# Routing logits with the gate as stationary operand, and combine weights turned in 32x32 blocks by VectorE

## The chip, the cores and the metric

The kernel runs on one core of one Trainium2 chip. The metric is the device time of one execution in microseconds (us); the value of a kernel is the median of its runs. A profile is one further execution, of which the hardware profiler keeps a trace with every instruction. The engines are called by the profile's names: PE is TensorE's matrix multiplications and PEld its weight loads, DVE is VectorE, ACT is ScalarE, POOL is GpSimd, and SP is SyncE, whose queue (SPq) issues most of the DMAs.

## The reference, cut to what matters

Eight sequences (B = 8) of 512 tokens (S) and 256 features (D) go through an attention layer and then through a mixture of 16 experts (E) with a hidden width of 128. Eight experts are kept for each token, and one shared expert is always added. What the change touches is the routing, here without the rest:

```
x = x + xattn(ctx_2048, layernorm(x), ...)
xf = layernorm(x)
logits = l2norm(xf) @ l2norm(gate_w).T        # 4096 tokens x 16 experts
scores = sigmoid(logits)
topk_scores, topk_idx = top_k(scores, 8)
combine = scores of the top 8 / their sum, 0 for the other experts
routed = sum over e of combine[:, e] * ((silu(xf @ w_gate[e]) * (xf @ w_up[e])) @ w_down[e])
out = x + routed + silu(xf @ sw_gate) * (xf @ sw_up) @ sw_down
```

## The kernel before

Every engine walks one list of steps, ORDER, and does its own part of each step; semaphores tie the engines together. The list is written out by hand: attention() gives each step a time by which the list is sorted, and order() appends the second half.

The first half is the attention: 16 groups of four heads (two groups for each sequence). A group's scores are computed twice on PE (L732 for the maxima, which DVE reduces at L1201, and L748 for the exponentials, which ACT takes at L868 into e_buf). POOL adds up the exponentials at L1407. The routing of sequence 0 and the first six expert units lie among the last groups.

The second half is the experts: units n = 0, 1, ... run over TODO, that is over 8 sequences b and 17 experts e (e = 16 is the shared one). A unit has a step gate_up (12 matmuls of 128x512 on PE, L840 through the helper at L653, into PSUM banks ps0 to ps3) and a step down (6 matmuls into pst). The step down of unit n stands behind gate_up of unit n + 2 (LAG = 2). In between, ACT computes silu into sg, DVE multiplies (L1304, and L1315 with the combine weight from CB), ACT rounds the product to hh (L868), and DVE takes the remainder hl (L1317). The operands are float32 kept as two float32r parts, a high one and a low one, so each product takes three matmuls.

The routing of sequence b + 1 is spread over the units of sequence b. After gate_up of e = 9 and 10 PE turns the normalized x (turn_x2), and X2h and X2l hold it with features on partitions. After gate_up of e = 12 PE computes the logits (L809 to L812), with 128 tokens of x as the stationary operand and the 16 or 32 gate columns moving. The 16 small DVE steps "gating" (N_GATE) follow: six of them after gate_up of e = 12, six after e = 13, the rest after e = 14. They put the two parts of the logits together (L1258, L1262), scale them (L1267), wait for ACT's tanh (L1270), find the eight largest (L1273, L1276), and leave the combine weights in LG, 128 tokens on partitions by 4 x 16. After gate_up of e = 15, the step turn_c turns LG on PE (four transposes), copies it with ACT to CT [16, 512], and SP stores CT to the scratch tensor in HBM with one DMA. From there, load_c brings one expert's row of 512 weights to all 128 partitions of a buffer of CB, of which there are NC = 4. The first four loads for a sequence stand right behind turn_c. A load of unit m waits until the DVE has used buffer m - 4.

For sequence 0 the same steps lie among the attention's groups 14 and 15, one at a time between other steps.

PSUM banks go round in rings: RING3 (three banks, first half) and RING2 (banks 4 and 5, second half) hold the steps that need a bank of their own; turn_c was one of them.

## Time and profile before

| | |
|---|---|
| device time, median of 3 runs | 1065.49 us (1064.21 to 1065.64) |
| span of the profiled execution, first to last instruction | 1056.2 us |
| PE busy | 1012.5 us, 96% of the span |
| DVE busy | 647.5 us, 61% |
| ACT busy | 465.9 us, 44% |
| POOL busy | 389.0 us, 37% |
| mean granted TensorE clock | 0.992 |

The profiled execution has no device time of its own on record, so its span is set beside the median of the runs: 9.3 us of the device time lie outside the span. A busy share is an average over both halves of the kernel. What the change is worth must be read in each half: where PE never waits, its own instructions set the time, and where it waits, the engine that it waits for does.

### The profile page before, as it was taken

How to read it: one execution, taken by the hardware profiler on the slowest of the kernel's cores; microseconds unless marked ns; L12 is line 12 of the kernel's file. 1: busy time of each engine (PE TensorE's matmuls, PEld its weight loads, DVE VectorE, ACT ScalarE, POOL GpSimd, SP SyncE). 2: the span in 40 equal slices, each digit the busy share in tenths (PEclk: the TensorE clock that was granted, in tenths of full speed). 3: DMA queues.
4: the chain of work that ended last, by engine and by line, in shares of the span. 5: the costliest groups of instructions: out<-in, count | busy, mean ns of one | idle time of the engine just before them, and what ended most of it. 6: DMA issues, size and time to landing. Idle time of an engine off the chain costs nothing.

```text
span 1056.2 us, 14941 instructions
## 1 busy us (share of the span) xinstructions
PE 1012.5 (96%) x5198; PEld 773.3 (73%) x5198; DVE 647.5 (61%) x1469; ACT 465.9 (44%) x865; POOL 389.0 (37%) x355
## 2 busy tenths in 40 slices
PE   4789999999999998899999999999999999999998
PEld 3656767676767665567888888888888888888886
DVE  5877777877777557355565555555555555555544
ACT  3346565656665646545323323333333333332322
POOL 3379797879797967345210010010010100100000
PEclk9899999999999999999999999999999999999999
DMA  7343433434333223324222121121220230221220
GB/s 239 104 131 78 131 81 111 108 84 131 73 110 75 65 65 105 92 86 131 75 80 61 52 80 50 61 81 40 72 80 31 71 90 20 91 80 31 93 68 20
DMA packets 65674, 87.87 MB, mean 83 GB/s; under 512 B 10720, under 2 KB 31088, under 8 KB 65600
## 3 DMA queue, kind: packets, MB, share of 16 engines
q1 hardware_dynamic: 63680, 84.83, 28.0%
q10 hardware_dynamic: 1920, 2.10, 0.6%
q8 instruction: 41, 0.67, 0.3%
q14 instruction: 33, 0.27, 0.1%
HBM read 56.97 MB, written 4.46 MB: 58 GB/s over the span
## 4 chain that ended last, share of the span: by engine, by line
PE 91%; DVE 4%; ACT 2%; SPq 1%; issue 1%; DMA 1%; POOL 0%; DVEq 0%; ACTq 0%
PE ps L653 50%; PE pst L653 18%; PE ps L732 6%; PE ps L759 5%; PE pst L748 5%; PE ps L659 4%; PE ps L772 1%; DVE mx L1201 1%; ACT e_buf L868 1%; SPq L606 1%; PE ps L811 1%; SPq L541 1%; ACT ctx_h L868 0%; DVE wsrc_l L1148 0%; PE ps L812 0%
## 5 line engine op out<-in xcount | busy, mean ns | idle before, releaser
L653 PE MATMUL ps<-x_h,weights 128*128 128x512 f32 x1088 | 365.6, 397 | 1.4 <-DVE x L1194 0.8
L653 PEld LDWEIGHTS ps<-x_h,weights 128*128 128x128 f32 x1088 | 204.5, 188 | 51.8 <-issue 1.0
L1201 DVE TENSOR_REDUCE mx<-ps 128x1 f32<-128x512 f32 x256 | 173.3, 685 | 81.8 <-PE ps L732 80.9
L868 ACT ACTIVATE hh<-qb 128x512 fp32r<-128x512 f32 x136 | 86.0, 632 | 296.4 <-DVE qb L1315 273.7
L653 PE MATMUL ps<-x_l,weights 128*128 128x512 f32 x544 | 214.6, 395 | 0.0
L653 PE MATMUL pst<-hh,weights 128*128 128x512 f32 x544 | 194.6, 399 | 0.0
L1304 DVE TENSOR_TENSOR qb<-ps,sg 128x512 f32<-128x512 f32 x136 | 94.1, 692 | 160.2 <-PE ps L653 153.8
L868 ACT ACTIVATE e_buf<-pst 128x512 f32<-128x512 f32 x256 | 147.4, 596 | 92.8 <-PE pst L748 81.8
L1317 DVE TENSOR_TENSOR hl<-qb,hh 128x512 fp32r<-128x512 f32 x136 | 94.3, 693 | 95.0 <-ACT hh L868 95.0
L1407 POOL TENSOR_TENSOR e_sums<-e_sums,e_buf 128x1024 f32<-128x1024 f32 x60 | 143.5, 2391 | 7.2 <-ACT e_buf L868 1.2
L1359 POOL TENSOR_SCALAR ve<-mv 128x4 f32<-128x4 f32 x8 | 1.8, 226 | 347.1 <-DVE mv L1242 347.1
L653 PEld LDWEIGHTS ps<-x_l,weights 128*128 128x128 f32 x544 | 102.1, 188 | 24.6
L748 PE MATMUL pst<-q_stack,k_stack 98*128 98x512 f32 x256 | 108.4, 425 | 12.1 <-ACT e_buf L868 12.0
L868 ACT ACTIVATE sg<-ps 128x512 f32<-128x512 f32 x136 | 81.1, 596 | 86.6 <-PE ps L653 86.6
L653 PEld LDWEIGHTS pst<-hh,weights 128*128 128x128 f32 x544 | 102.2, 188 | 23.3 <-DVE hl L1317 0.8
L732 PE MATMUL ps<-k_stack,q_stack 97*128 97x512 f32 x256 | 109.7, 430 | 6.7 <-DVE mx L1201 6.2
L653 PE MATMUL pst<-hl,weights 128*128 128x512 f32 x272 | 107.3, 394 | 0.0
L1315 DVE TENSOR_TENSOR qb<-qb,cb 128x512 f32<-128x512 f32 x124 | 87.4, 705 | 4.2
L1407 POOL TENSOR_TENSOR e_sums<-e_buf 128x1024 f32<-128x1024 f32 x30 | 71.8, 2394 | 48.8 <-PE ps L772 48.3
L732 PEld LDWEIGHTS ps<-k_stack,q_stack 97*128 97x128 f32 x256 | 49.2, 193 | 46.0 <-issue 29.1
L748 PEld LDWEIGHTS pst<-q_stack,k_stack 98*128 98x128 f32 x256 | 49.4, 194 | 27.1 <-ACT e_buf L868 16.6
L759 PE MATMUL ps<-e_buf,v_buf 128*32 128x512 f32 x512 | 62.1, 603 | 0.0
(159 smaller groups left out, 1391.5 us busy)
## 6 DMA issues: line engine op xcount, KB each, us to landing
cb<-combine_scratch SPq DMA_DIRECT2D x128, 256.0 KB, 3.2
q_stack<-q_h SPq DMA_DIRECT2D x128, 64.0 KB, 2.0
k_stack<-k_h SPq DMA_DIRECT2D x124, 64.0 KB, 2.0
ctx_raw<-in_ctxT SPq DMA_DIRECT2D x7, 1024.0 KB, 5.2
q_stack<-q_l SPq DMA_DIRECT2D x64, 64.0 KB, 2.0
out_x<-ob SPq DMA_DIRECT2D x16, 256.0 KB, 2.2
k_stack<-k_l SPq DMA_DIRECT2D x62, 64.0 KB, 2.0
x<-in_x SPq DMA_DIRECT2D x7, 512.0 KB, 6.5
```

The costliest lines, as they stand in the source:

```text
L541: e.dma_start(f32(KS[g % 2][at:at + 32, h, :]), f32(src[32 * h:32 * h + 32, :])).then_inc(sem(f"stack{g % 2}{h}"), 16)
L653: ins = engine.matmul(dst, lhsT, rhs, start=start and n == 0, stop=stop and n == len(terms) - 1)
L659: ins = engine.transpose(dst, src, ID[0:k, 0:k])
L732: engine.matmul(ps, QS[z][0:97, h, 128 * q:128 * q + 128], KS[z][0:97, h, :], start=True, stop=True).then_inc(sem("s_max"), 1)
L748: engine.matmul(YP[:, m % 2, :], KS[z][0:98, h, 128 * k:128 * k + 128], QS[z][0:98, h, :], start=True, stop=True).then_inc(sem("s_t"), 1)
L759: ins = engine.matmul(OP[32 * i:32 * i + 32, :], VB[:, b % 2, k, hh + i, :], EB[:, SLOTS[8 * g + 4 * (i // 2) + k], i % 2, :], start=k == ...
L868: return engine.activation(dst, src, func, **kw)
L1201: engine.tensor_reduce(MX[:, g % 2, h // 2, h % 2, q:q + 1], bank(step), AX.X, ALU.max).then_inc(sem("max"), 1)
L1304: engine.tensor_tensor(QB[:, w, :], GP[n][1], SG[:, w, :], ALU.mult).then_inc(sem("hq"), 1)
L1315: engine.tensor_tensor(QB[:, w, :], QB[:, w, :], CB[:, m % NC, :], ALU.mult).then_inc(sem("hc"), 1)
L1317: engine.tensor_tensor(HLB[:, n % NH, :], QB[:, w, :], f32(HHB[:, n % NH, :]), ALU.subtract).then_inc(sem("h_lo"), 1)
L1407: engine.tensor_tensor(ES[:, a, :, :], first, EB[:, SLOTS[n + 1 + i], :, :], ALU.add).then_inc(sem("e_add"), 1)
```

## The change

The logits are now computed with the gate as the stationary operand: GT holds four copies side by side of the 32 columns (16 high parts, 16 low parts), 128 columns in all, and the 512 tokens of a sequence move. That is four matmuls of 128x512 instead of sixteen of 128x32 or 128x16. The result has the gate's columns on partitions, four times over, and the tokens along the free axis. Four DVE transposes in 32x32 blocks, one for each group of 32 partitions, each read a quarter of the tokens and put them on partitions in LT; one DVE addition joins the high and the low part. That makes 19 gating steps instead of 16, and since the steps are handed out six at a time after e = 12, 13 and 14, one is left for e = 15.

The step turn_c loses its PE transposes and its ACT copy. One DVE transpose in 32x32 blocks turns LG into CT [128, 2, 32] instead, and because the blocks leave the experts of different token blocks on different partitions, SP stores CT with eight DMAs in place of one, in runs of 32 numbers (128 bytes). The loads from the scratch tensor are as before, but wait for all eight stores. The gate's rows, as loaded, now lie in a free part of shift_rows.

```diff
@@ sizes, rings, tiles
-N_LN1, N_LN2, N_GROWS, N_GATE = N_SMALL1 + 4, N_SMALL2 + 4, 3 + rsqrt_steps(1) + 3, 16
+N_LN1, N_LN2, N_GROWS, N_GATE = N_SMALL1 + 4, N_SMALL2 + 4, 3 + rsqrt_steps(1) + 3, 19
-         if s[0] in ("q", "y", "shift", "turn_x", "turn_s", "turn_r", "turn_x2", "turn_c", "bo")
+         if s[0] in ("q", "y", "shift", "turn_x", "turn_s", "turn_r", "turn_x2", "bo")
-         if s[0] in ("turn_x2", "turn_c", "store") or (s[0] == "gating" and s[2] == 0)]
+         if s[0] in ("turn_x2", "store") or (s[0] == "gating" and s[2] == 0)]
-        GT = sb("gate_t", [128, 2, 2, E], F32R)
+        GT = sb("gate_t", [128, 2, 4, 2, E], F32R)
-        CT = s2("ct", [E, S])
+        LT, CT = s2("lt", [128, 4, 2 * E]), s2("ct", [128, 2, 32])
@@ SyncE
                     sp.wait_ge(sem("ct"), b + 1)
-                    engine.dma_start(cscr[b], CT[:, :]).then_inc(sem("st_ct"), 16)
+                    for r in range(4):
+                        for c in range(2):
+                            at = 32 * r + E * c
+                            engine.dma_start(cscr[b].rearrange("e (a c r t) -> e a c r t", a=2, c=2, r=4)[:, :, c, r, :],
+                                             CT[at:at + E, :, :]).then_inc(sem("st_ct"), 16)
@@ TensorE
-                    lp = own_bank(step)[:, 0:8 * E].rearrange("p (q e) -> p q e", q=4)
-                    for q in range(4):
-                        tok = slice(128 * q, 128 * q + 128)
-                        both = GT[:, :, :, :].rearrange("p k a e -> p k (a e)")
-                        engine.matmul(lp[:, q, :], X2h[:, b % 2, 0, tok], both[:, 0, :], start=True, stop=False)
-                        for k in range(2):
-                            engine.matmul(lp[:, q, 0:E], X2l[:, b % 2, k, tok], GT[:, k, 0, :], start=False, stop=False)
-                        ins = engine.matmul(lp[:, q, :], X2h[:, b % 2, 1, tok], both[:, 1, :], start=False, stop=True)
+                    lp = own_bank(step)
+                    for k in range(2):
+                        four = GT[:, k].rearrange("p f a e -> p (f a e)")
+                        engine.matmul(lp, four, X2h[:, b % 2, k, :], start=k == 0, stop=False)
+                        ins = engine.matmul(lp, four, X2l[:, b % 2, k, :], start=False, stop=k == 1)
                     ins.then_inc(sem("logit"), 1)
-                elif kind == "turn_c":
-                    b = step[1]
-                    pe.wait_ge(sem("gating"), N_GATE * (b + 1))
-                    ps = own_bank(step)
-                    turns([(ps[0:E, 128 * q:128 * q + 128], LG[:, q, :]) for q in range(4)], sem("c_t"))
@@ ScalarE
-                elif kind == "turn_c":
-                    b = step[1]
-                    act.wait_ge(sem("c_t"), b + 1)
-                    if b > 0:
-                        act.wait_ge(sem("st_ct"), 16 * b)
-                    copy(CT[:, :], bank(step)[0:E, :]).then_inc(sem("ct"), 1)
@@ VectorE
-                    if i == 0:
-                        lp = bank(step)[:, 0:8 * E].rearrange("p (q a e) -> p q a e", q=4, a=2)
-                        dve.wait_ge(sem("logit"), b + 1)
-                        if b > 0:
-                            dve.wait_ge(sem("c_t"), b)
-                        engine.tensor_copy(LG[:, :, :], lp[:, :, 1, :]).then_inc(done, 1)
-                    elif i == 1:
-                        lp = bank(("gating", b, 0))[:, 0:8 * E].rearrange("p (q a e) -> p q a e", q=4, a=2)
-                        dve.wait_ge(done, base + 1)
-                        engine.tensor_tensor(LG[:, :, :], lp[:, :, 0, :], LG[:, :, :], ALU.add).then_inc(done, 1)
+                    if i < 4:
+                        r = slice(32 * i, 32 * i + 32)
+                        lp = bank(("gating", b, 0)).rearrange("p (q r t) -> p q r t", q=4, r=4)
+                        if i == 0:
+                            dve.wait_ge(sem("logit"), b + 1)
+                        engine.transpose(LT[r, :, :], lp[r, :, i, :]).then_inc(done, 1)
+                    elif i == 4:
+                        dve.wait_ge(done, base + 4)
+                        engine.tensor_tensor(LG[:, :, :], LT[:, :, 0:E], LT[:, :, E:2 * E], ALU.add).then_inc(done, 1)
...
+                elif kind == "turn_c":
+                    b = step[1]
+                    dve.wait_ge(sem("gating"), N_GATE * (b + 1))
+                    if b > 0:
+                        dve.wait_ge(sem("st_ct"), 128 * b)
+                    engine.transpose(CT[:, :, :], LG[:, :, :].rearrange("p (a c) e -> p a (c e)", a=2)).then_inc(sem("ct"), 1)
```

Three places show what moves in the lists of the engines. The first is DVE in the second half, at the routing of sequence 1, before the change, from the unit e = 14 to the unit e = 15 (qb, hh and hl are the unit's products, cb the combine weight, lg the logits and later the weights):

```order
L1317 TENSOR_TENSOR hl<-qb,hh 128x512 [waits h_hi]
L1278 TENSOR_REDUCE ts_57<-t_56 128x4
L1281 RECIPROCAL ts_57<-ts_57 128x4 [waits gating]
L1283 TENSOR_TENSOR sc<-sc,rep 128x64
L1286 TENSOR_TENSOR lg<-sc,ts_57 128x64 [waits gating]
L1304 TENSOR_TENSOR qb<-ps,sg 128x512 [waits h_lo,silu,gu]
L1315 TENSOR_TENSOR qb<-qb,cb 128x512 [waits ld_cb3,hq]
L1317 TENSOR_TENSOR hl<-qb,hh 128x512 [waits h_hi]
```

The same place of DVE in the changed kernel:

```order
L1272 TENSOR_TENSOR sc<-sc,rep 128x64
L1299 TENSOR_TENSOR qb<-ps,sg 128x512 [waits h_lo,silu,gu]
L1310 TENSOR_TENSOR qb<-qb,cb 128x512 [waits ld_cb3,hq]
L1312 TENSOR_TENSOR hl<-qb,hh 128x512 [waits h_hi]
L1275 TENSOR_TENSOR lg<-sc,ts_57 128x64 [waits gating]
L1282 STREAM_TRANSPOSE ct<-lg 128x64 [waits st_ct,gating]
L1299 TENSOR_TENSOR qb<-ps,sg 128x512 [waits h_lo,silu,gu]
```

The last gating step has moved behind the unit e = 15, and the turn stands behind it.

The second place is SP's queue behind that step, before the change:

```order
L628 DMA combine_scratch<-ct 16x512 [waits ct]
L635 DMA cb<-combine_scratch 128x512 [waits hc,st_ct]
```

And in the changed kernel, at the routing of sequence 0, the same two steps (the next four rows of the queue, word for word):

```order
L629 DMA combine_scratch<-ct 32x1x32 [waits ct]
L629 DMA combine_scratch<-ct 32x1x32 x7
L637 DMA cb<-combine_scratch 128x512 [waits st_ct]
L637 DMA cb<-combine_scratch 128x512 x3
L551 DMA w_raw<-in_wg 128x2x128 [waits w_lo]
```

Seven more stores stand in front of the first load.

The third place is DVE at the routing of sequence 0, in the attention's last but one group, before the change (mx is a maximum of scores, ru the reciprocals of the sums, rn the scale of the logits):

```order
L1258 COPY lg<-ps 128x64 [waits logit]
L1262 TENSOR_TENSOR lg<-ps,lg 128x64 [waits gating]
L1201 TENSOR_REDUCE mx<-ps 128x1 [waits s_max]
L1267 TENSOR_TENSOR lg<-lg,rn 128x64 [waits ln2,gating]
L1207 RECIPROCAL ru<-ps 128x16 [waits spread,s_turned]
L1270 TENSOR_SCALAR sc<-sc 128x64 [waits tanh]
```

The same place in the changed kernel:

```order
L1248 STREAM_TRANSPOSE lt<-ps 32x128 [waits logit]
L1248 STREAM_TRANSPOSE lt<-ps 32x128
L1190 TENSOR_REDUCE mx<-ps 128x1 [waits s_max]
L1248 STREAM_TRANSPOSE lt<-ps 32x128
L1196 RECIPROCAL ru<-ps 128x16 [waits spread,s_turned]
L1248 STREAM_TRANSPOSE lt<-ps 32x128
L1251 TENSOR_TENSOR lg<-lt 128x64 [waits gating]
L1190 TENSOR_REDUCE mx<-ps 128x1 [waits s_max]
L1256 TENSOR_TENSOR lg<-lg,rn 128x64 [waits ln2,gating]
L1259 TENSOR_SCALAR sc<-sc 128x64 [waits tanh]
```

The addition that joins the two parts read one operand from PSUM and now reads both from SBUF (lt), and a reduction stands between it and the scaling.

## Rows read from the trace of the kernel before

**Rows 1.** Windows: stretch, length, then busy us of PE, PEld, DVE, ACT, POOL; PEclk.

```profile
478.00:1050.00 572.00, 572.00 (x2589) 463.92 (x2588) 315.50 (x617) 192.13 (x336) 47.96 (x134) 1.00 0.21 66
```

**Rows 2.** Timeline, routing of sequence 0: start, us, engine, line, instruction, idle before.

```profile
410.55 2.35 POOL L1407 TENSOR_TENSOR e_sums<-e_sums,e_buf 128x1024 f32<-128x1024 f32 x1
...
411.18 1.80 DVE L1267 TENSOR_TENSOR lg<-lg,rn 128x64 f32<-128x64 f32 x1
412.86 1.27 POOL L1431 TENSOR_TENSOR weights<-w_raw,weights 128x512 fp32r<-128x512 f32 x1
...
413.01 0.26 ACT L868 ACTIVATE sc<-lg 128x64 f32<-128x64 f32 x1 [2.43 <-DVE lg L1267]
...
413.90 0.59 PE L748 MATMUL pst<-q_stack,k_stack 98*128 98x512 f32 x1 [2.46 <-ACT e_buf L868]
...
419.69 0.81 DVE L1286 TENSOR_TENSOR lg<-sc,ts 128x64 f32<-128x64 f32 x1
```

**Rows 3.** Timeline of PE, logits of sequence 7.

```profile
955.08 0.39 PE L653 MATMUL ps<-x_h,weights 128*128 128x512 f32 x1
...
957.01 0.48 PE L653 MATMUL pst<-hh,weights 128*128 128x512 f32 x1
957.33 0.39 PE L653 MATMUL pst<-hl,weights 128*128 128x512 f32 x1
```

**Rows 4.** Timeline of PE, turning the combine weights of sequence 7.

```profile
969.44 0.39 PE L653 MATMUL ps<-x_h,weights 128*128 128x512 f32 x1
969.67 0.60 PE L659 MATMUL ps<-ident_sb,lg 128*16 128x128 f32 x4
...
970.34 0.40 PE L653 MATMUL pst<-hl,weights 128*128 128x512 f32 x1
```

**Rows 5.** Groups by line and form, DVE: busy us, mean ns, idle before.

```profile
L1304 DVE TENSOR_TENSOR qb<-ps,sg 128x512 f32<-128x512 f32 x136 | 94.1, 692 | 160.2 <-PE ps L653 153.8 <-ACT sg L868 5.8
...
L1262 DVE TENSOR_TENSOR lg<-ps,lg 128x64 f32<-128x64 f32 x8 | 1.8, 224 | 0.3
...
L1258 DVE COPY lg<-ps 128x64 f32<-128x64 f32 x8 | 1.8, 219 | 1.0 <-PE ps L812 1.0
```

**Rows 6.** Timeline of DVE, first units of sequence 7.

```profile
979.42 0.69 DVE L1315 TENSOR_TENSOR qb<-qb,cb 128x512 f32<-128x512 f32 x1
980.82 0.69 DVE L1317 TENSOR_TENSOR hl<-qb,hh 128x512 fp32r<-128x512 f32 x1 [0.70 <-ACT hh L868]
...
987.09 0.69 DVE L1304 TENSOR_TENSOR qb<-ps,sg 128x512 f32<-128x512 f32 x1 [0.78 <-PE ps L653]
```

**Rows 7.** Timeline of all engines, the end of the routing of sequence 7.

```profile
969.87 0.69 DVE L1304 TENSOR_TENSOR qb<-ps,sg 128x512 f32<-128x512 f32 x1 [0.69 <-PE ps L653]
...
971.86 0.57 ACT L868 ACTIVATE ct<-ps 16x512 f32<-16x512 f32 x1
```

**Rows 8.** Timeline of SP's queue, the loads that follow.

```profile
974.03 14.82 SPq L635 DMA_DIRECT2D cb<-combine_scratch  x7
```

**Rows 9.** DMA issues: KB each, median us from issue to landing.

```profile
cb<-combine_scratch SPq DMA_DIRECT2D x128, 256.0 KB, 3.2
...
out_x<-ob SPq DMA_DIRECT2D x16, 256.0 KB, 2.2
...
combine_scratch<-ct SPq DMA_DIRECT2D x8, 32.0 KB, 1.6
```

**Rows 10.** Line 641, the output's stores: issue ns min/median/max, first and last start.

```profile
L641 SPq DMA_DIRECT2D out_x<-ob x16: 388/389/389, 543.2 to 1053.6; - x16
```

**Rows 11.** Line 628, the store of CT, the same columns.

```profile
L628 SPq DMA_DIRECT2D combine_scratch<-ct x8: 317/318/341, 422.5 to 972.5; - x8
```

**Rows 12.** Line 606, copies into the stacks, the same columns.

```profile
L606 SPq DMA_DIRECT2D q_stack<-q_h x128: 507/590/1601, 22.5 to 403.6; - x128
```

**Rows 13.** Timeline of all engines, the first combine weights of sequence 0.

```profile
425.48 1.77 SPq L635 DMA_DIRECT2D cb<-combine_scratch  x4
...
432.89 0.69 DVE L1309 SCALAR_TENSOR_TENSOR qb<-qb,cb 128x512 f32<-128x512 f32 x1
```

More of the change, by code:

```diff
@@ L477, in bank_free @@
             if kind == "gating":
-                return sem("gating"), N_GATE * s[1] + 2
-            if kind == "turn_c":
-                return sem("ct"), COUNT[s]
+                return sem("gating"), N_GATE * s[1] + 4
             return sem("o_add"), COUNT[s]
@@ L988, in scalar_program @@
                     gb = bank(step)[:, 0:2 * E].rearrange("p (k e) -> p k e", k=2)
-                    copy(GT[:, :, 0, :], gb).then_inc(sem("gate_hi"), 1)
+                    four = gb.rearrange("p k (f e) -> p k f e", f=1).to_broadcast([128, 2, 4, E])
+                    copy(GT[:, :, :, 0, :], four).then_inc(sem("gate_hi"), 1)
                 elif kind == "second_starts":
@@ L1232, in vector_program @@
                         dve.wait_ge(sem("gate_hi"), 1)
-                        engine.tensor_tensor(GT[:, :, 1, :], gb, f32(GT[:, :, 0, :]), ALU.subtract).then_inc(sem("gate_lo"), 1)
+                        four = gb.rearrange("p k (f e) -> p k f e", f=1).to_broadcast([128, 2, 4, E])
+                        engine.tensor_tensor(GT[:, :, :, 1, :], four, f32(GT[:, :, :, 0, :]), ALU.subtract).then_inc(sem("gate_lo"), 1)
                 elif kind == "ln2" and (step[2] < 8 or 10 <= step[2] < 12):
@@ L1270, in vector_program @@
                         engine.tensor_scalar(SC[:, :, :], SC[:, :, :], 0.5, 0.5, ALU.mult, ALU.add).then_inc(done, 1)
-                    elif i < 8:
-                        dve.wait_ge(done, base + 4)
-                        engine.max(T8[:, i - 4, :], SC[:, i - 4, :]).then_inc(done, 1)
-                    elif i < 12:
-                        dve.wait_ge(done, base + 8)
-                        engine.match_replace(REP[:, i - 8, :], T8[:, i - 8, :], SC[:, i - 8, :], 0.0).then_inc(done, 1)
-                    elif i == 12:
+                    elif i < 11:
+                        dve.wait_ge(done, base + 7)
+                        engine.max(T8[:, i - 7, :], SC[:, i - 7, :]).then_inc(done, 1)
+                    elif i < 15:
+                        dve.wait_ge(done, base + 11)
+                        engine.match_replace(REP[:, i - 11, :], T8[:, i - 11, :], SC[:, i - 11, :], 0.0).then_inc(done, 1)
+                    elif i == 15:
@@ L1278, in vector_program @@
                         engine.tensor_reduce(TS8[:, :, :], T8[:, :, :], AX.X, ALU.add).then_inc(done, 1)
-                    elif i == 13:
-                        dve.wait_ge(done, base + 13)
+                    elif i == 16:
+                        dve.wait_ge(done, base + 16)
                         engine.reciprocal(TS8[:, :, :], TS8[:, :, :]).then_inc(done, 1)
-                    elif i == 14:
+                    elif i == 17:
                         engine.tensor_tensor(SC[:, :, :], SC[:, :, :], REP[:, :, :], ALU.subtract).then_inc(done, 1)
-                    elif i == 15:
-                        dve.wait_ge(done, base + 15)
+                    elif i == 18:
+                        dve.wait_ge(done, base + 18)
```

16 lines of the change are left out of this document (8 added, 8 removed).

## The prediction

> **What bounds the kernel now.** I read the windows of the trace first, because the busy shares of the page are means over two different halves. In the experts' half PE is busy for 572.00 of 572.00 us, at a granted clock of 1.00 (the 2.4 GHz level); DVE is busy for 55% and ACT for 34% of it [rows 1]. So in this half time is worth what PE's own instructions cost, and work on another engine is free as long as PE does not come to wait for it. Then I read the timeline around the change's places. The reader is to look at distances between starts, not at durations: matmuls overlap, and a packed 128x512 matmul starts 0.23 us after the one before it, although its row says 0.39. At sequence 0 the kernel is another: there, in the attention, PE waited 2.46 us at 413.90 us, and the wait leads through ACT's tanh (which waited 2.43 us, and behind which the exponentials stand in ACT's order) to DVE's scaling of the logits, which took 1.80 us [rows 2].
>
> **The logits on PE, experts' half.** Between the last full matmul of the unit e = 12 (start 955.08) and the second one behind the logits (957.33) lie 2.25 us [rows 3]. Two packed steps take 0.47 of that, so the sixteen small matmuls cost 1.78 us, 0.11 each: none is paid by its 16 or 32 columns. They become four matmuls of 128x512, the same shape and types as the experts' (x parts moving, 128 stationary columns), and 4 x 0.233 = 0.93 us. Gain: 0.85 us.
>
> **The turn on PE.** From 969.44 to 970.34 us are 0.90 us for four transposes and two packed steps [rows 4]: 0.43 us, all of which goes. Together 1.28 us for each sequence. Seven of the eight sequences (1 to 7) are routed in the half where PE never waits: 7 x 1.28 = 9.0 us.
>
> **DVE, experts' half.** The trace shows no DVE transpose. Below, its price is bounded by the copy from PSUM of half the elements, 219 ns for 128x64. From that and the 692 ns of 128x512 [rows 5] comes a slope of 1.06 ns per element of a partition, so 128 elements a partition would take 0.29 us; above I take the whole 692 ns. A cost by elements is the natural reading of these rows, and I use 0.29: four make 1.15 us, against the copy and the addition that go (0.44 us). The new addition and the turn of LG are 128x64 (0.22 us each). Net 1.15 us more for a sequence. After e = 12 the chain of six steps is then 1.15 + 2 x 0.22 and some gaps, about 1.7 us. A unit lasts 4.2 us: L1315 of e = 0 starts at 979.42 and L1304 of e = 2 at 987.09 [rows 6], and with the 0.69 us of the L1304 ahead of L1315 [rows 5] two units make 8.4 us. DVE, waiting for ACT in the middle, is tied up from 978.70 (that L1304) to 981.51 (the end of hl), 2.8 us of it. So 1.4 us are left per unit, 0.93 more where the logits run, and the tanh for ACT falls about when silu of the next unit is due. What overruns is a few tenths and is late only for hq and hl, which PE needs late: down of a unit starts behind gate_up of the unit after next, at about 986.9 us for the product whose hl ends at 981.51 [rows 6]. That cover is 5.4 us. With 0.69 us for a transpose the overrun is 1.6 us more, still under it. ACT loses its copy of 0.57 us [rows 7]. I cost all of this at nothing.
>
> **The store and the loads, experts' half.** This is the longest new chain. Before, CT was ready at 972.43, 2.56 us after the start of the product of e = 15 at 969.87 [rows 7], and the first loads were issued at 974.03 [rows 8]. Landing 3.2 us later [rows 9] makes 977.2, and the first use is at 979.42 [rows 6]: 2.2 us to spare, 1.8 once PE's turn is gone. Now the last gating step and the turn stand behind hl of e = 15 (2.8 us, then 2 x 0.22 and gaps): CT is ready at about 3.4, that is 0.85 us later. Eight issues take seven more of them: by the output's stores, also SBUF to HBM with three dimensions, 0.39 us [rows 10] and 0.03 between them (my choice, as the rows show none back to back), 2.9 us; the ends are the old store's own 0.32 us [rows 11] and the 0.59 us of the copies into the stacks [rows 12]. Landing: 2.2 instead of 1.6 us [rows 9], ends 1.6 and the double of 2.2. The weights come 0.85 + 2.9 + 0.6 = 4.35 us later and DVE waits 2.6 us for them, at L1315's place of e = 0. Ends: 0.85 + 2.45 = 3.3 us later (a wait of 1.5) and 0.85 + 4.3 + 2.8 = 7.9 (a wait of 6.1). Behind the waiting product stand hl, the next unit's product, and on ACT hh and the next silu; PE waits for hl only after 5.4 us. So the expected wait of 2.6 us is paid off over two units by the 1.4 us that each has left, and costs nothing; the high end costs 0.7 us a sequence, 5 us in all.
>
> The Trainium skill speaks against exactly this part: its page "DMA: Bandwidth & Descriptors" (section Specifications) says that transfers under 512 B are done as read-modify-write, and the new runs have 128 B. It gives no duration for such a store, so it would add an unknown time to the landing, and the sum stays as it is unless that passes the cover; no row here shows such a store.
>
> **Sequence 0.** Here DVE is on the path. The scaling (128x64, both operands in SBUF) ran from 411.18 to 412.98, eight times its usual 0.22 us, and ended when POOL's addition of 410.55 + 2.35 = 412.90 did [rows 2]. The addition before it, which reads PSUM, took its usual 224 ns (its group's mean [rows 5]) although POOL ran as well. After the change both the addition and the scaling read only SBUF. The addition would then end with POOL's instruction at 412.9, the reduction behind it takes 0.69, and the scaling meets POOL's next instruction, which ends at 412.86 + 1.27 = 414.13 [rows 2]: the logits are ready at about 414.3 instead of 412.98, and PE's wait ends 1.3 us later. The 0.85 us that the logits save lies ahead of this wait and only lengthens it; the 0.43 us of the turn is behind it and counts. Net +0.9 us. Ends: -1.3, if the additions fall between POOL's instructions and PE's whole saving counts, and +4, if one more of the DVE steps that follow meets a POOL addition of 2.35 us and another of 1.27. The weights for unit 0 need no more time than there is: from the end of lg at 420.50 [rows 2], a reduction and the turn make about 421.4, the stores and their landing 2.9 + 0.4 + 2.2, so 426.9 instead of the loads' issue at 425.48, landing 430.1 to 430.5; the use is at 432.89 [rows 13].
>
> The Trainium skill's page "SBUF — State Buffer" (section SBUF: two separate sides) has the rule: VectorE with two SBUF inputs and GpSimd share one port pair, and the loser is blocked for the whole instruction. The row of 1.80 us agrees. [...]
>
> **Sum.** -9.0 + 0.9 = -8.1 us. The profiled span is 1056.2 us, and 9.3 us lie around it up to the median of the runs, 1065.5; the change does not touch these. 1065.5 - 8.1 = **1057.4 us**, a ratio of 0.992.
>
> **The rivals.**
> 1. *The weights come late.* The chain of eight stores passes the cover, and PE waits in every sequence. For it: seven issues in one queue, short runs. Against it: the dearest of the three issues shown has a median of 0.59 us, and the two stores to HBM land after 1.6 and 2.2 us [rows 9, 12]. The cover ends when the weights come 1.8 + 5.4 = 7.2 us later than now; each us beyond that costs 7 us, so the gain of 8.1 is gone at 8.4 us later. With 9.5 us: 7 x 2.3 = 16 us, 1057.4 + 16 = 1073.5. This is the rival on the other side. 6%.
> 2. *Sequence 0 pays more.* The lock between DVE and POOL hits several steps, PE waits 3 to 6 us more there: 1060 to 1063.5 us. The chain at 411 to 414 us speaks for it, and the next POOL instructions leave few gaps. 14%.
> 3. *Sequence 0 pays nothing*: PE's saving counts eight times and the steps fall into gaps. 1065.5 - 10.3 = 1055.2 us. 15%.
> 4. *The transpose is slow*, at or above 0.69 us: absorbed in the experts' half, but sequence 0 gets 4 x 0.4 = 1.6 us more on its path: 1059 us. 10%.
> 5. *The change doesn't save on PE*: matmuls that read the fourfold gate do not run at 0.23 us. Nothing in the profile says so, since the experts' matmuls have the same shape. With twice the price (0.47 us each) the logits cost what they did, and 3 us remain from the turn: 1063.4 us. 4%.
>
> **How the numbers follow.** The forecast's own case, with sequence 0 between 0 and +2 us, has 51% and lies at 1056.3 to 1058.8. Rivals 2, 3 and 4 border on it. Leaving out rivals 1 and 5 and the far tail of 2 leaves out under 2 in 10: 1054.6 to 1062.0. A measurement of this kernel tells about 0.2% (2.1 us) from no change. Faster by more than that takes all cases but rival 1, half of 5 and the last of 2: 0.90. Within it 0.04, slower 0.06.
>
> **What the profile of the changed kernel would show.** Right: PE packed in the experts' half, four 128x512 matmuls 0.23 us apart in each routing and no matmul for the turn; the half shorter by 9.0 us. DVE transposes of 0.29 us. At e = 0 of each sequence DVE waits about 2.6 us for the DMA of cb, and PE does not wait for hl. At sequence 0 a scaling or an addition of over 1 us beside a POOL instruction. It would be wrong if PE's waits list hl or qb in the experts' half, if issues of the new stores take over 0.7 us, or if the wait at sequence 0 grows past 4 us.

## The result, and the profile after

The changed kernel takes 1091.34 us (median; 1089.9 to 1094.46) against 1064.85 us (1063.19 to 1065.64) for the kernel before on the same chip: a ratio of 1.0263, 95% interval 1.0237 to 1.0289. The prediction said 1057.4 us and faster; the kernel is 26.5 us slower. What happened is rival 1 in kind, the weights come late and PE waits in every sequence, but from a smaller lateness than rival 1 asked for: it let PE wait only when DVE waits longer than 5.4 us for the weights, and DVE waited 4.0 us on average (5.6 at sequence 1).

I read the waits of the experts' half first, since the forecast stood on PE not waiting there. In the kernel before, PE was busy for all of [rows 1]. After:

```profile
DVE qb L1310 <- DMA cb<-combine_scratch: 27.9, 7, 5.6
...
PE pst L655 <- DVE yt L1320: 22.5, 7, 5.1
```

(Waits: engine, line, what it waited for, us in total, times, longest.) DVE waits seven times for the combine weights, 4.0 us each (predicted: 2.6), and PE waits seven times, 3.2 us each, for something that the prediction never named: yt, the copy of the *finished* sequence's output out of PSUM. (The load of PE's weights for the same step, on PEld, is put down to hl, 25.4 us in 7. At sequence 7 that hl is the one of unit 1, which ended at 1022.09 and which down of e = 0 doesn't need; the hl that it needs had ended at 1019.38.) (Lines have moved: L655, L1299, L1310, L1312 and L1320 are the L653, L1304, L1315, L1317 and L1325 of before; L629 stores CT, L637 loads the weights.)

The timeline shows how the two waits hang together. These are the last unit of routing for sequence 7 and the first units of sequence 7, of the changed kernel:

```profile
1004.50 0.69 DVE L1299 TENSOR_TENSOR qb<-ps,sg 128x512 f32<-128x512 f32 x1 [0.53 <-PE ps L655]
...
1007.48 0.25 DVE L1282 STREAM_TRANSPOSE ct<-lg 128x64 f32<-128x64 f32 x1
1007.76 4.99 SPq L629 DMA_DIRECT2D combine_scratch<-ct  x8
...
1012.89 0.69 DVE L1299 TENSOR_TENSOR qb<-ps,sg 128x512 f32<-128x512 f32 x1 [2.11 <-PE ps L655]
1013.94 10.43 SPq L637 DMA_DIRECT2D cb<-combine_scratch  x7
1017.30 0.69 DVE L1310 TENSOR_TENSOR qb<-qb,cb 128x512 f32<-128x512 f32 x1 [3.72 <-DMA cb<-combine_scratch]
...
1018.69 0.69 DVE L1312 TENSOR_TENSOR hl<-qb,hh 128x512 fp32r<-128x512 f32 x1 [0.70 <-ACT hh L862]
...
1021.28 0.58 ACT L862 ACTIVATE yt<-pst 128x512 f32<-128x512 f32 x1
1021.40 0.69 DVE L1312 TENSOR_TENSOR hl<-qb,hh 128x512 fp32r<-128x512 f32 x1 [0.70 <-ACT hh L862]
...
1022.01 0.69 DVE L1320 COPY yt<-pst 128x512 f32<-128x512 f32 x1
...
1022.85 0.47 PE L655 MATMUL pst<-hh,weights 128*128 128x512 f32 x1 [1.61 <-DVE yt L1320]
```

Read it from the bottom. PE's down of e = 0 writes the PSUM banks pst, in which the sequence before is still lying until yt0 (ACT) and yt1 (DVE) have been copied out. Both copies belong to the step down of the shared expert, and that step stands in ORDER behind gate_up of e = 1. So on DVE the copy comes behind the product that waits for the weights (1017.30), behind its hl (1018.69), and behind all of unit 1 (up to 1022.1). What PE needs *of unit 0* was ready at 1019.38; it started at 1022.85.

The next rows answer to the other rows of before. First PE's logits of sequence 7 (x moving, four matmuls, then down of the unit), to be read beside [rows 3]:

```profile
990.56 0.40 PE L655 MATMUL ps<-x_h,weights 128*128 128x512 f32 x1
990.79 0.40 PE L810 MATMUL ps<-x_h,gate_t 128*128 128x512 f32 x1
...
991.73 0.39 PE L655 MATMUL pst<-hh,weights 128*128 128x512 f32 x1
991.96 0.40 PE L655 MATMUL pst<-hl,weights 128*128 128x512 f32 x1
```

From 990.56 to 991.96 are 1.40 us where [rows 3] had 2.25: 0.85 us saved. DVE's new operations in the experts' half (groups by form: busy, mean ns), to be read beside [rows 5]:

```profile
L1248 DVE STREAM_TRANSPOSE lt<-ps 32x128 f32<-32x128 f32 x28 | 8.7, 311 | 0.7
L1282 DVE STREAM_TRANSPOSE ct<-lg 128x64 f32<-128x64 f32 x7 | 1.7, 246 | 0.2
L1251 DVE TENSOR_TENSOR lg<-lt 128x64 f32<-128x64 f32 x7 | 1.6, 226 | 0.2
```

The stores (line statistics: issue min/median/max ns), to be read beside [rows 10 to 12]; their landing had a median of 1.8 us:

```profile
L629 SPq DMA_DIRECT2D combine_scratch<-ct x64: 552/592/1626, 428.9 to 1012.2; - x64
```

**PE's clock after the waits.** PE's granted clock has two levels in these traces, 1.00 (2.4 GHz) and 0.50 (1.2 GHz); a value between them is a window that holds both. Windows (stretch, length, busy us of PE, PEld, DVE, ACT, POOL, granted clock, DMA share, GB/s) of the whole half, of 6 us behind the wait of 3.11 us of sequence 6, and of 6 us around the wait of 1.61 us of sequence 7:

```profile
484.00:1086.00 602.00, 578.69 (x2498) 464.80 (x2497) 323.73 (x647) 189.86 (x336) 47.65 (x139) 0.98 0.21 63
...
944.00:950.00 6.00, 4.23 (x13) 3.43 (x14) 3.79 (x11) 1.63 (x4) 1.43 (x7) 0.72 0.31 90
1020.00:1026.00 6.00, 4.39 (x20) 3.27 (x19) 3.97 (x6) 2.33 (x5) 0.00 (x0) 1.00 0.31 89
```

[Rows 1] had 1.00. Six of the seven waits, 3.0 to 5.1 us long, were followed by a stretch at the 1.2 GHz level; the seventh, of 1.61 us, was not. The windows of 10 us around the first five waits have 0.66 once and 0.83 four times, and the window shown of the sixth 0.72: that is 3.4 + 4 x 1.7 + 1.7 = 11.9 us lost at most, since a small part of these stretches fell into the waits.

**Where the time went.** The start of hl in unit 3 of sequence 0 and in the last unit (timelines; the kernel before, then the changed one):

```profile
458.15 0.69 DVE L1317 TENSOR_TENSOR hl<-qb,hh 128x512 fp32r<-128x512 f32 x1 [0.69 <-ACT hh L868]
...
1048.05 0.69 DVE L1317 TENSOR_TENSOR hl<-qb,hh 128x512 fp32r<-128x512 f32 x1 [0.70 <-ACT hh L868]
```

```profile
469.12 0.69 DVE L1312 TENSOR_TENSOR hl<-qb,hh 128x512 fp32r<-128x512 f32 x1 [0.70 <-ACT hh L862]
...
1084.07 0.69 DVE L1312 TENSOR_TENSOR hl<-qb,hh 128x512 fp32r<-128x512 f32 x1 [0.70 <-ACT hh L862]
```

They lie 589.90 us apart before and 614.95 us in the changed kernel. So this stretch is 25.05 us longer: -9.0 (PE's saving, seven times 1.28) + 22.5 (waits for yt) leaves 11.5, and the clock behind the waits, at most 11.9 us, accounts for nearly all of that. Ahead of that stretch the changed kernel is 10.97 us later, of which 3.55 us arise in the first 101 us (by a wait of PE that ends at 101.04 before and at 104.59 after), 4.65 up to unit 0, and 2.8 between units 1 and 2. The first part was between 2.1 and 4.4 us in all profiles that have the new turn and -0.6 in the one without it (e1, below); whether the turn or chance makes it stays open. The third part is PE's clock: the windows from 449 to 458 us have 0.62 in the changed kernel and 1.00 in e4 (below), whose code is the same up to there, so it isn't the change's. The profiles' spans differ by 36.0 us and the medians by 26.5, because the profiled execution of before, with the 2.2 us that lie around a span, took 1058.4 us, 6.4 below its median, and that of the changed kernel 1094.5, 3.1 above its own. (The executions of before differ by PE's clock: of those beside experiments 9 and 10, the shortest, 1058.97 us, had a mean granted clock of 0.990 and the longest, 1066.37, had 0.984; the profiled one had 0.992.) What follows compares medians, or stretches inside the traces.

### The profile page after: what moved, and what is told of

It reads as the page before. It is cut to its first block, busy times and chain, and to the rows that moved or that the text cites. A ratio compares the mean times of both kernels' runs of the same rounds, so it can differ in the third digit from the quotient of the medians.

```text
span 1092.2 us, 14757 instructions
## 1 busy us (share of the span) xinstructions
PE 1020.6 (93%) x5070; PEld 773.9 (71%) x5070; DVE 655.9 (60%) x1501; ACT 459.6 (42%) x857; POOL 386.9 (35%) x355
## 4 chain that ended last, share of the span: by engine, by line
PE 76%; DVE 9%; SPq 4%; ACT 4%; DMA 4%; issue 3%; POOL 0%; DVEq 0%; ACTq 0%
PE ps L655 41%; PE pst L655 14%; PE ps L761 5%; PE ps L734 5%; PE pst L750 5%; PE ps L661 4%; SPq L629 3%; DMA cb<-combine_scratch 2%; DVE qb L1310 2%; DVE qb L1299 1%; DMA combine_scratch<-ct 1%; PE ps L774 1%; ACT hh L862 1%; DVE mx L1190 1%; DVE st L1229 1%
## 5 line engine op out<-in xcount | busy, mean ns | idle before, releaser
L655 PE MATMUL ps<-x_h,weights 128*128 128x512 f32 x1088 | 367.8, 399 | 1.4 <-DVE x L1183 0.8
L655 PEld LDWEIGHTS ps<-x_h,weights 128*128 128x128 f32 x1088 | 206.3, 190 | 52.5 <-issue 1.0
L655 PE MATMUL pst<-hh,weights 128*128 128x512 f32 x544 | 199.2, 408 | 22.5 <-DVE yt L1320 22.5
L655 PE MATMUL ps<-x_l,weights 128*128 128x512 f32 x544 | 215.6, 396 | 0.0
L1299 DVE TENSOR_TENSOR qb<-ps,sg 128x512 f32<-128x512 f32 x136 | 93.8, 690 | 152.1 <-PE ps L655 139.2
L1312 DVE TENSOR_TENSOR hl<-qb,hh 128x512 fp32r<-128x512 f32 x136 | 94.2, 693 | 95.0 <-ACT hh L862 95.0
L655 PEld LDWEIGHTS pst<-hh,weights 128*128 128x128 f32 x544 | 105.0, 193 | 49.7 <-DVE hl L1312 26.2
L655 PEld LDWEIGHTS ps<-x_l,weights 128*128 128x128 f32 x544 | 103.3, 190 | 25.3
L655 PE MATMUL pst<-hl,weights 128*128 128x512 f32 x272 | 110.1, 405 | 0.0
L1310 DVE TENSOR_TENSOR qb<-qb,cb 128x512 f32<-128x512 f32 x124 | 87.7, 707 | 31.9 <-DMA cb<-combine_scratch 27.9
```

The lines of the kernel that those rows point to most:

```text
L655: ins = engine.matmul(dst, lhsT, rhs, start=start and n == 0, stop=stop and n == len(terms) - 1)
L1299: engine.tensor_tensor(QB[:, w, :], GP[n][1], SG[:, w, :], ALU.mult).then_inc(sem("hq"), 1)
L1310: engine.tensor_tensor(QB[:, w, :], QB[:, w, :], CB[:, m % NC, :], ALU.mult).then_inc(sem("hc"), 1)
L1312: engine.tensor_tensor(HLB[:, n % NH, :], QB[:, w, :], f32(HHB[:, n % NH, :]), ALU.subtract).then_inc(sem("h_lo"), 1)
```

## The experiments

Theory A: PE's terms are right, and the kernel is slow because the chain of stores makes the weights late, and lateness beyond about 2 us reaches PE through the yt copies. Theory B: something else in the change is dear (the new logits, DVE's load), or it is the stores' way to memory. The kernel before had a median of 1063.67 us beside experiments 1 to 4, 1063.63 beside 5 to 8, and 1065.29 beside 9 and 10.

### 1 and 2. Each half of the change alone

e1_logits_only: the changed kernel with before's turn (PE, ACT, one store of [16, 512]), and seven gating steps in each of the units 12 to 14.

```diff
+                    engine.dma_start(cscr[b], CT[:, :]).then_inc(sem("st_ct"), 16)
...
+                    turns([(ps[0:E, 128 * q:128 * q + 128], LG[:, q, :]) for q in range(4)], sem("c_t"))
...
+                    copy(CT[:, :], bank(step)[0:E, :]).then_inc(sem("ct"), 1)
...
-                    engine.transpose(CT[:, :, :], LG[:, :, :].rearrange("p (a c) e -> p a (c e)", a=2)).then_inc(sem("ct"), 1)
```

> The new logits alone: gate stationary, DVE transposes and the addition from SBUF as in the change, but PE transposes, ACT copy and one store for the combine weights as before (seven gating steps per unit, so that all 19 are done after e = 14). Theory 'stores': the loss of the change comes from the eight stores, so here PE saves 0.85 us in each sequence and sequence 0 gives back 1.3 us or more: 1057 to 1062 us, no wait of PE for yt in the experts' half. Rival 'DVE and lock': the DVE transposes and the SBUF addition cost the time: 1070 us or more.

e2_turn_only: the kernel before with the new turn (one DVE transpose, eight stores) and its old logits.

> The new turn alone: the logits as before, LG turned by DVE and stored with eight DMAs. Theory 'stores': the whole loss is here. DVE waits 5 to 6 us for cb at e = 0 of sequences 1 to 7, PE waits 3 to 5 us for yt in each and runs at half clock for some us behind it: 1085 to 1098 us. Rival 'DVE and lock': 1060 to 1067 us.

Measured: e1 1059.99 us (1058.64 to 1062.28), ratio 0.9975 (0.9961 to 0.9989), no wait for yt. e2 1093.98 us (1087.45 to 1095.53), ratio 1.0277 (1.0248 to 1.0306), PE's waits for yt 19.9 us in 7, DVE's for cb 25.3 us in 7. The whole loss comes with the turn and its stores; the logits alone gain, and with DVE's transposes in place.

### 3. One store in place of eight

e3_one_store: the changed kernel; CT is stored by one DMA in the order in which it lies, in runs of 256 bytes. It leaves out the sorting of the weights, which reach the experts in another order; the number of bytes and all other work are the same.

```diff
-                    for r in range(4):
-                        for c in range(2):
...
+                    engine.dma_start(cscr[b].rearrange("e (x f) -> (e x) f", f=64),
+                                     CT[:, :, :].rearrange("p a t -> p (a t)")).then_inc(sem("st_ct"), 16)
```

> The changed kernel, with CT stored by one DMA in its own layout in place of eight (the combine weights reach the experts in a wrong order, so the routed part of the output is another; all other work is the same). Theory 'stores', by their issue in one queue: the weights come about 4 us earlier than in the changed kernel, PE never waits for yt: 1055 to 1062 us. Rival 'place of the turn' (the last gating step and the turn behind the unit e = 15 are late enough by themselves): still over 1070 us.

Measured: 1059.02 us (1057.32 to 1059.91), ratio 0.9958 (0.9941 to 0.9974); no wait for yt; the store's issue 0.32 us, its landing 1.4. DVE's transposes, at the same place in its order, cost nothing in the experts' half: what costs is the eight stores.

### 4. The same eight stores, one unit earlier

e4_early_turn: seven gating steps in each of the units 12 to 14 in place of six, and turn, stores and loads behind unit 14.

```diff
-                    run(c, 6)
-                if e == 15:
+                    run(c, 7)
+                if e == 14:
```

> The changed kernel with seven gating steps per unit and the turn, its eight stores and the loads moved one unit earlier (behind e = 14). Theory 'stores': 4.2 us earlier is enough to take the wait off PE, which needs the yt copy; DVE still waits some us for cb: 1055 to 1063 us. Rival 'stores landing': if the short stores disturb the loads or the landing is what takes the time, part of the waits stays: 1068 us or more.

Measured: 1062.17 us (1059.04 to 1064.28), ratio 0.9984 (0.9970 to 0.9998); PE's waits for yt 2.8 us in 2. Two lines of the order give back 29 us with all eight stores still there, so what costs is not the stores as such but when they end.

### 5 and 6. Issue or landing, by the store or by the piece

e5_two_queues: four of the eight stores are issued from ACT's queue. e6_four_stores: four stores of 32 partitions, each with two experts' groups c, the same 128-byte runs.

```diff
-                        for c in range(2):
-                            at = 32 * r + E * c
-                            engine.dma_start(cscr[b].rearrange("e (a c r t) -> e a c r t", a=2, c=2, r=4)[:, :, c, r, :],
-                                             CT[at:at + E, :, :]).then_inc(sem("st_ct"), 16)
+                        engine.dma_start(cscr[b].rearrange("e (a c r t) -> c e a r t", a=2, c=2, r=4)[:, :, :, r, :],
+                                         CT[32 * r:32 * r + 32, :, :]).then_inc(sem("st_ct"), 16)
```

> The changed kernel, with four of the eight small stores issued from ScalarE's queue at once with the other four on SyncE's. The stores, their sizes and what waits for them are the same. Theory A (the loads are late by the time that one queue needs to issue eight stores, 5.8 us, and all lateness over about 2 us reaches TensorE through the yt copy): SyncE issues four in 2.9 us, the loads go out 2 to 3 us sooner, the waits of TensorE's down product for yt fall from 22.5 us to 2 to 10 us, and the time is 1064 to 1078 us. ScalarE's own work behind its four issues comes later, which may give back a part. Theory B (the stores' way to memory is the slow thing, not their issue): the loads go out within 1 us of where they did, and the time stays at 1087 to 1095 us.

> The changed kernel, with four stores of 32 partitions each in place of eight of 16: the same bytes, in the same pieces of 128 bytes, at the same places in memory, at the changed kernel's place in the order. Theory A (an issue costs about 0.73 us for each store, whatever it holds, and lateness over about 2 us is paid in full): the loads go out some 2.9 us sooner, TensorE's waits for yt fall from 22.5 us to 1 to 6 us, and the time is 1060 to 1069 us. Theory B (an issue costs by the pieces in it): each of the four takes about 1.4 us, nothing moves, and the time is 1087 to 1095 us.

Measured: e5 1071.25 us (1065.61 to 1072.94), ratio 1.0066 (1.0044 to 1.0088); e6 1067.81 us (1064.24 to 1069.43), ratio 1.0037 (1.0015 to 1.0058). SP's queue at the turn for sequence 1 (timelines; start, time of the group of issues): the changed kernel,

```profile
533.09 5.81 SPq L629 DMA_DIRECT2D combine_scratch<-ct  x8
540.08 11.78 SPq L637 DMA_DIRECT2D cb<-combine_scratch  x7
```

the one with two queues (ACT issued its four in the same 3.28 us),

```profile
532.59 3.28 SPq L629 DMA_DIRECT2D combine_scratch<-ct  x4
537.39 12.09 SPq L637 DMA_DIRECT2D cb<-combine_scratch  x7
```

the one with four stores,

```profile
532.83 2.46 SPq L627 DMA_DIRECT2D combine_scratch<-ct  x4
536.66 11.80 SPq L635 DMA_DIRECT2D cb<-combine_scratch  x7
```

and the one with one store:

```profile
532.41 0.32 SPq L626 DMA_DIRECT2D combine_scratch<-ct  x1
533.85 12.55 SPq L634 DMA_DIRECT2D cb<-combine_scratch  x7
```

From the first store to the first load are 6.99, 4.80, 3.83 and 1.44 us (at sequence 2, where no issue is longer than the rest, 6.18, 3.95 and 3.85 for the first three). All but 1.1 to 1.5 us of each is issue, so the queue's time is the lever and not the landing; and four stores with twice the pieces each take 0.61 us apiece, no more than the eight (0.62 to 0.73), so among these stores an issue is paid by the store and not by its pieces. It isn't the same for every store: the one store of e3, which has a plain layout, took 0.32. PE's waits for yt follow: 22.5 us in 7, 7.8 in 6, 6.2 in 6, none. In e5 the four issues hold ACT up: at sequence 2 its next silu started 4.67 us after the hh before it (613.11 and 608.44), against 1.34 in the changed kernel (613.20 and 611.86). DVE waited 38.3 us for silu in the experts' half of e5 and 12.7 in that of e6, but that hardly reached PE (next paragraph).

The Trainium skill's page "Perfetto Trace Analysis" (section DMA Optimizations) says that balancing DMAs across the engines that can issue them may help when generating the descriptors is the bottleneck. e5 agrees by its 20 us. Fewer stores on one queue did 3.4 us more, and in the profiles that lies at sequence 1 alone: there SP's four issues took 3.28 us in e5 against 2.46 at the later sequences, the loads left 1.0 us later than in e6, PE waited 3.20 us against 1.93, and only in e5 a stretch at the 1.2 GHz level followed. At the others PE's waits are alike (0.80 to 1.05 us in e5, 0.69 to 1.05 in e6), so ACT's lateness cost next to nothing.

### 7 and 8. Sequence 0, and the best version

e7_old_first: e4, with sequence 0 alone computing its logits as before the change. e8_all_three: e7 with the four stores of e6.

```diff
+                    if b == 0:
...
+                            engine.matmul(old[:, q, :], X2h[:, 0, 0, tok], both[0], start=True, stop=False)
...
+                    if b == 0 and i < 5:
...
+                            engine.tensor_copy(LG[:, q, :], lp[:, q, 1, :]).then_inc(done, 1)
```

> The kernel with the turn and the stores one unit earlier, with sequence 0 alone computing its logits as before the change (16 matmuls with x stationary, one copy and one add in halves, no 32x32 transposes); the other seven sequences have the new form. Theory A (the four transposes and the slow add beside GpSimd's work bring sequence 0's routing some 1.3 us late, and TensorE's wait for them brings a stretch at half clock, 4.6 us together): sequence 0's lateness falls by 3 to 5 us against the kernel without this edit, whose median was 1062.17 us, and the time is 1056.5 to 1060 us. Theory B (the 4.6 us come from elsewhere in the first half, such as the rewritten gate tables, and vary by themselves): no fall, 1061 to 1064 us.

> The best version that the theories point to: turn and stores one unit earlier, four stores of 32 partitions in place of eight of 16, and sequence 0's logits as before the change. Theory A: no waits of TensorE for yt are left (2.8 us in the kernel with the early turn alone), all of the 1.28 us for each of seven sequences is kept, sequence 0 loses nothing: 1063.67 - 9 = 1054.7, so 1053 to 1058 us. If an issue costs by its pieces and not by the store, the third edit gives nothing and the time is that of the kernel with old logits in sequence 0, 1056.5 to 1060 us. If sequence 0's lateness is not from the new logits either, 1060 to 1063 us.

Measured: e7 1057.79 us (1055.6 to 1058.26), ratio 0.9946 (0.9925 to 0.9966). e8 1054.56 us (1052.65 to 1056.23), ratio 0.9921 (0.9896 to 0.9947): faster than both kernels. Counted from the wait of PE at 101 us, unit 0 of sequence 0 comes 1.9 us later than in the kernel before, in e7 and e8 alike, where it came 4.65 us later in the changed kernel and 4.6 in e3 and e4. So 2.7 us of the loss are the new logits in sequence 0, a little less than the 3 expected at least. The medians of e4 and e7 differ by more, 4.4 us; in their profiles PE's waits for yt fall from 2.8 to 2.1 us as well, and the stretch at the 1.2 GHz level behind e4's wait of 2.2 us is gone. Where the 1.9 us that stay lie, the traces show: from the end of PE's wait for the exponentials to unit 0 are 18.27 us before and 20.09 in e7, at a mean granted clock of 0.91 and 0.87, and in e7 PE waits 1.06 us for a maximum (mx) on DVE that it doesn't wait for in the kernel before. The first and the last hl of e8, to be read beside those above:

```profile
462.44 0.69 DVE L1330 TENSOR_TENSOR hl<-qb,hh 128x512 fp32r<-128x512 f32 x1 [0.70 <-ACT hh L869]
...
1043.27 0.69 DVE L1330 TENSOR_TENSOR hl<-qb,hh 128x512 fp32r<-128x512 f32 x1 [0.70 <-ACT hh L869]
```

580.83 us against 589.90 before: 9.07 us less, and the prediction's -9.0 for PE is met when nothing waits.

### 9 and 10. The copies moved, the weights left late

e9_early_yt: the changed kernel, its eight stores where they were; only the two copies stand ahead of the elementwise work of unit 1 (on ACT behind its silu). e10_all_four: e8 with the same move.

```diff
+                    if b > 0 and e == 1:
+                        dve.wait_ge(sem("dn"), n - 1)
...
+                        engine.tensor_copy(YT[:, 1, :], YP[:, 1, :]).then_inc(sem("yt1"), 1)
                     dve.wait_ge(sem("gu"), 2 * n + 2)
```

> The changed kernel with its eight stores where they are, and one thing moved: the two copies of the finished sequence's output from PSUM (yt, one on ScalarE, one on VectorE) stand before the elementwise work of unit 1 of the next sequence, not behind it. The combine weights come as late as in the changed kernel, 6.1 us. Theory A (the late weights hold TensorE only through the yt copies, which stand behind the waiting multiply of unit 0; what TensorE itself needs of unit 0, its hl, still comes about 1.9 us before the down product would start): TensorE's waits for yt, 22.5 us in 7, nearly vanish though VectorE still waits some 25 us for the weights, the half-clock stretches behind them go too, and the time is 1057 to 1063 us. Theory B (lateness of 6 us reaches TensorE by hl or by the buffers of the gate and up products anyway): the waits move to another line and the time stays above 1075 us.

> The fastest version so far (turn one unit earlier, four stores of 32 partitions, sequence 0's logits as before the change; 1054.56 us) with the yt copies moved as well. That version's trace has no wait of TensorE for yt in the seven turns between sequences. Theory A (the copies' place matters only when the weights are late): the same time within 0.3%, 1052 to 1057 us. Theory B (the copies' place costs by itself, or gains): outside of that.

Measured: e9 1063.02 us (1058.74 to 1065.82), ratio 0.9988 (0.9968 to 1.0007). e10 1055.22 us (1054.5 to 1056.81), ratio 0.9916 (0.9894 to 0.9939), the same as e8. Waits of e9 in the experts' half:

```profile
DVE qb L1320 <- DMA cb<-combine_scratch: 27.9, 7, 5.6
PE pst L655 <- DVE yt L1300: 3.0, 3, 2.1
```

and its timeline at sequence 7:

```profile
988.83 0.69 DVE L1320 TENSOR_TENSOR qb<-qb,cb 128x512 f32<-128x512 f32 x1 [3.54 <-DMA cb<-combine_scratch]
...
990.22 0.69 DVE L1322 TENSOR_TENSOR hl<-qb,hh 128x512 fp32r<-128x512 f32 x1 [0.70 <-ACT hh L862]
990.56 0.59 ACT L862 ACTIVATE yt<-pst 128x512 f32<-128x512 f32 x1
990.83 0.68 DVE L1300 COPY yt<-pst 128x512 f32<-128x512 f32 x1
```

DVE waits for the weights as long as in the changed kernel, 27.9 us, and PE waits 3.0 us in all (at sequence 7 not at all: down of e = 0 starts at 992.78, 1.3 us after the copy ends), and its clock stays at 1.00 through the half. So the link is shown: against one store, where nothing is late, the lateness costs 32 us with the copies behind unit 1 (1091.34 against 1059.02), and 3 to 4 us with the copies ahead of it (ratio 0.9988 against 0.9958; the median lies 0.02 us above what was expected). Once the weights are in time the copies' place is worth nothing (e10).

## Why the prediction was wrong, point by point

**PE's terms: right.** 0.85 us for the logits is in the trace, and 9.07 us for seven sequences are in e8; without the waits PE is 9 us faster, as said.

**DVE's price: right.** 0.29 us was chosen for a transpose of 128 elements a partition and 311 ns measured; the turn and the addition 246 and 226 ns against 0.22; all of it hidden (e3). The Trainium skill's page "VectorE: DVE Perf Modes" (section The three transpose paths) gives 311 ns for a VectorE transpose of a 128x128 bf16 tile. No run here has that shape or type; the 32x128 f32 block read from PSUM took the same 311 ns, the 128x64 one 246.

**The cover of 5.4 us: the step that failed.** The prediction listed what stands behind the waiting product as "hl, the next unit's product, and on ACT hh and the next silu", and let PE wait only for hl. It left out the copies of yt, behind unit 1's work on DVE and ACT, for which down of e = 0 waits as well. The trace of before had it (timeline, sequence 7):

```profile
982.89 0.69 DVE L1304 TENSOR_TENSOR qb<-ps,sg 128x512 f32<-128x512 f32 x1 [1.39 <-PE ps L653]
...
985.62 0.68 DVE L1325 COPY yt<-pst 128x512 f32<-128x512 f32 x1
...
986.89 0.40 PE L653 MATMUL pst<-hh,weights 128*128 128x512 f32 x1
```

The copy ended at 986.30 and that down started at 986.89, 0.59 us of room. DVE's idle time between the product at 979.42 and that copy adds the 1.39 us in which it waited for PE. True cover: 2.0 us, and 0.2 in the six sequences that have a next one, where the statistics of the next layer norm use it up (timeline of before, sequence 6):

```profile
906.17 1.40 DVE L1239 BATCH_NORM_STATS2 st<-x 128x6 f32<-128x256 f32 x4
...
910.37 0.37 DVE L1242 BATCH_NORM_AGGREGATE mv<-st 128x2 f32<-128x6 f32 x4
910.65 0.66 DVE L1325 COPY yt<-pst 128x512 f32<-128x512 f32 x1
```

A check by sequence 7: DVE's wait of 3.72 - 2.0 = 1.7, measured 1.61; by sequence 6: 3.65 - 0.2 = 3.4, measured 3.11. Even the predicted wait of 2.6 us would have cost 6 x 2.4 + 0.6 = 15 us and turned the sign. e9 shows how the tightest waiter moves. This is its sequence 1, where DVE waited 5.58 us for the weights:

```profile
543.81 0.69 DVE L1322 TENSOR_TENSOR hl<-qb,hh 128x512 fp32r<-128x512 f32 x1 [0.70 <-ACT hh L862]
544.42 1.40 DVE L1234 BATCH_NORM_STATS2 st<-x 128x6 f32<-128x256 f32 x4
545.73 0.67 DVE L1300 COPY yt<-pst 128x512 f32<-128x512 f32 x1
546.55 0.47 PE L655 MATMUL pst<-hh,weights 128*128 128x512 f32 x1 [2.06 <-DVE yt L1300]
```

PE still waits for the copy, which now stands behind hl and the statistics: a cover of 5.6 - 2.1 = 3.5 us, which is the predicted 5.4 less the 1.3 and 0.6 that these two take. The 5.4 for hl fits this row (hl ended at 544.50, when PE had just run out of work), but no run has hl as the last to come.

**The lateness: mis-sized by 1.4 us.** CT was ready 3.23 us after the start of the product of e = 15 (predicted 3.4). Eight issues took 5.0 to 5.8 us, 0.62 to 0.73 each, against 3.3 (0.39 and 0.03 between them); the upper end taken from the stacks' copies (0.59) would have been near. Landing 1.8 us against 2.2. The rule on transfers under 512 B, which the prediction cites from the Trainium skill's page "DMA: Bandwidth & Descriptors" (section Specifications), shows little cost in the landing here: runs of 128 B landed after 1.8 us, the old store after 1.6 [rows 9].

**What a wait brings with it: missing.** No term stood for PE's clock after a wait; it is nearly all of the 11.5 us that the waits of 22.5 us leave in a stretch that is 25.05 us longer.

**Sequence 0: right in kind, too small.** Logits ready 1.3 us later and a net of +0.9 us were predicted. Ready they were 1.3 us later (417.84 against 412.98, less the 3.55 us of the start). The routing beside POOL's additions, changed kernel:

```profile
414.20 2.34 POOL L1402 TENSOR_TENSOR e_sums<-e_sums,e_buf 128x1024 f32<-128x1024 f32 x1
...
415.22 1.40 DVE L1251 TENSOR_TENSOR lg<-lt 128x64 f32<-128x64 f32 x1
416.50 1.26 POOL L1426 TENSOR_TENSOR weights<-w_raw,weights 128x512 fp32r<-128x512 f32 x1
...
417.26 0.58 DVE L1256 TENSOR_TENSOR lg<-lg,rn 128x64 f32<-128x64 f32 x1
...
417.87 0.26 ACT L862 ACTIVATE sc<-lg 128x64 f32<-128x64 f32 x1 [4.45 <-DVE lg L1256]
...
418.76 0.77 PE L750 MATMUL pst<-q_stack,k_stack 98*128 98x512 f32 x1 [4.59 <-ACT e_buf L862]
```

The addition ends with POOL's instruction (416.6) and the scaling meets the next, as predicted. PE then waits 4.59 us, 2.13 more than in [rows 2]; less the 0.85 that the logits save, that is the predicted 1.3. What the prediction lacked comes behind this wait: it had only the -0.43 of the turn there, and the way from the wait's end to unit 0 grew from 18.27 to 21.62 us, with 1.52 us of waiting for a maximum on DVE that before had not, and a mean granted clock of 0.83 against 0.91. The net was 4.65 us up to unit 0. This was rival 2, given 14%; by itself it would not have changed the sign. e7 confirms 2.7 us of it. Why PE comes to wait for the maximum isn't settled.

**The span: read wrongly.** "9.3 us lie around the span" set one execution's span against the median of others. In the profiles that have their own device time the two differ by 2.2 to 2.3 us, in e5 by 2.6; the other 7 were the luck of one execution at a high clock. It did not decide anything here.

**Rivals and chances.** Rival 1 was priced with a threshold of 7.2 us of lateness, from the false cover. With the true one it begins at 2.0, below the expected 4.35, so it would have been the forecast. Of the three signs of being wrong that the prediction named, two came, both at the edge: the eight issues took 0.73 us each at sequence 1 (0.62 at most others), and the wait at sequence 0 was 4.59 us. The third looked for PE waiting for hl or qb, and it was yt. A chance of 6% rested on one list of waiters being complete.

## What to carry to other kernels

Before a late transfer is costed at nothing, list *everything* that stands behind the waiting instruction on its engine up to the next use by the bounding engine, with steps that belong to other units or to the item before, such as copies that free a PSUM bank; the tightest of them is the cover, not the one that the data flow suggests. A step that splits one DMA into several is paid by the issue, one after another in its queue: use fewer and bigger ones, or put the step earlier. And where the bounding engine works without a gap, count its clock too: here six waits of 21 us together cost some 11 us more behind them.

## What the runs showed of the hardware

- Small stores SBUF to HBM in runs of 128 bytes, issued back to back from SP: 0.61 to 0.73 us each in the experts' half, with 16 partitions (4 KB) or 32 (8 KB) alike; a single store of 32 KB in runs of 256 bytes (e3) or 2 KB (before) 0.32 us.
- DVE's 32x32 transpose of a 32x128 f32 block from PSUM took 311 ns, of 128x64 from SBUF 246 ns.
- In the experts' half, where PE had run at a granted clock of 1.00, waits of 3.0 to 5.1 us (the changed kernel, e2, e5) were each followed by a stretch at the 1.2 GHz level. Shorter ones went either way: in e2 one of 2.0 us was followed by such a stretch (clock 0.55 from 1022 to 1024 us) and one of 2.88 us was not (1.00 from 538 to 560 us); one of 2.2 us (e4) was, those of 2.1 us (e9), 1.9 us (e6) and 1.61 us were not. The attention's last wait of 2.47 us before unit 2 was followed by one in the changed kernel and not in e4.
